# The mix of five paths: its weighing moved from GpSimd to VectorE

## The chip, the cores and the metric

The kernel runs on one core of one Trainium2 chip. The metric is the device time of one execution in microseconds (us), taken as the median of several runs. Engines: TensorE (PE, with its weight loads as PEld), VectorE (DVE), ScalarE (ACT), GpSimd (POOL) and SyncE (SP), which here only issues transfers. Each engine works through its own queue in order; the queues meet in semaphores.

## The reference

A layer on x of shape (2, 1024, 256): a spiking front, a gated attention, a recurrence and a mixture of experts. The change lies in the end of the attention, which for each of 2048 tokens and each of 4 heads mixes five paths of 64 values with weights from a softmax, normalizes, and projects:

```python
probs = jax.nn.softmax(logits / tau[:, None], -1)
eps = jax.nn.sigmoid(eps_logit) * 0.2
probs = probs * (1.0 - jnp.sum(eps, -1, keepdims=True)) + eps
o = jnp.einsum('blhp,blhpd->blhd', probs, paths)
o = o * jax.lax.rsqrt(jnp.mean(o * o, -1, keepdims=True) + 1e-05) * norm_w
return o.reshape(b, Ln, D) @ Wo
```

The logits come from a small network on the hidden states and on four statistics of each path (mean, mean square, mean absolute value, norm).

## The kernel before, in words

The function `mix` treats the tokens as 16 tiles of 128 (a = 0 to 15), four of them to a chunk (n = 0 to 3, TILES = 4, CHUNKS = 4). `m.path[:, a]` holds for one tile 128 tokens x 5 paths x 256 values, so 1280 values in each partition. Each engine has its own list of steps; nothing but the order in these lists and the semaphores decides what runs when.

VectorE, for a tile: `sums` (L1353) makes the statistics; three reductions, over 512 values each for tiles 0 to 11 (part of their statistics was made earlier) and over 1280 for tiles 12 to 15. For a chunk: `scores` (L1363) and `probs` (L1378) make the softmax around ScalarE's exp and leave the weights in `pr[n % 2]`, releasing `probs_ready`. `combine` (L1394) waits for the tile's weighing (`weighted`) and adds the five weighted paths in three additions (L1398, L1400, L1404), releasing `mixed`. `squares` (L1406), `normed` (L1415) do the normalization around ScalarE's Square and Sqrt (`root`, L1186), and `residual` (L1426) adds the projected result to x.

GpSimd, before: nothing but the weighing. For each tile it waits for its chunk's `probs_ready` and multiplies the tile's 1280 values by the weights in place (L1158).

The order on VectorE is written out: in round i, the sums of chunk i + 1, then combine, squares and normed of chunk i - 1, then residual of chunk i - 2, then scores(i) and probs(i). So between probs(n) and combine of chunk n lie, for n = 0 and 1, the twelve reductions of chunk n + 2. For n = 2 nothing lies between. After the last round comes a tail: combine(12), combine(13), residual(2), squares(3), combine(14), combine(15), normed(3), squares(4), normed(4), residual(3), residual(4). From PARTS = ((0, 4), (4, 8), (8, 12), (12, 14), (14, 16)), squares, normed, root, project and residual take chunk 3 in two parts, numbered 3 and 4.

ScalarE in round i: `st_out` (L1168, copies the transposed statistics of chunk i), four `gelu` with the squares of the next chunk between them, `turned_back(i - 2)` (copies for the projection), `norm`, `root(i - 1)`, and the exp of chunk i. Its tail: turned_back(2), zw_out(0), rows_out(0), root(3), zw_out(1), rows_out(1), root(4) and so on.

TensorE in round i: `hidden(i)` (needs st_out(i)), `project(i - 2)`, `logits(i)` (L1277, writes `lg_bank` for scores(i)). Its tail: project(2), gate_part(0), rows(0), gate_part(1), rows(1), project(3), gate_part(2), rows(2), project(4), rows(3), gate_part(3). project(x) transposes the normalized part (L1290) and multiplies by Wo (L1299); gate_part (L1313) and rows (L1329) prepare the recurrence that follows. The recurrence begins when all engines have finished `mix`.

Of the kernel before, what the change touches and what calls it, by code (L numbers as in the profile page):

```python
# [15 lines left out]
ALU = mybir.AluOpType  # L16
# [3 lines left out]
P = 128  # L20
# [3 lines left out]
H, DV = 4, 64  # L24
NP = 5
# [8 lines left out]
CHUNKS = T // CH  # L34
# [1040 lines left out]
def mix(nc, d, m):  # L1075
# [8 lines left out]
    TILES = N // P  # L1084
    CHUNKS = B * T // N
# [5 lines left out]
    with ExitStack() as own:  # L1091
# [11 lines left out]
        pr = [sb(f"pr{i}", [P, TILES, H, NP]) for i in range(2)]  # L1103
# [16 lines left out]
        s = namedtuple("MixSemaphores", names)(*(sem("m_" + n) for n in names))  # L1120
        row_bank = (st_bank, lg_bank)
        path = lambda a: m.path[:, a]
# [3 lines left out]
        block = own.enter_context(nc.Block())  # L1126

        @block.sync
        def _(sp):
            for x in (*m.done_in_project, *m.done_in_fir):  # L1130
                sp.sem_clear(x)
            sp.dma_start(b2[:], d.gb2.partition_broadcast(P)).then_inc(s.g_in, 16)
            sp.dma_start(w2[:], d.gW2.rearrange("(f p) n -> p f n", p=P)).then_inc(s.g_in, 16)
            sp.dma_start(wo[:], d.Wo.rearrange("(c p) n -> p c n", p=P)).then_inc(s.g_in, 16)
            for h in range(P // DV):
                sp.dma_start(nw[h * DV:(h + 1) * DV, :], d.norm_w.unsqueeze(1)).then_inc(s.g_in, 16)
            for c in range(C):
                sp.dma_start(m.xT[:, c * B:(c + 1) * B, :], d.xT[c * P:(c + 1) * P]).then_inc(s.x_in, 16)
            sp.dma_start(m.bias_g[:], d.bg).then_inc(s.wg_in, 16)
            sp.dma_start(m.alpha[:], d.alpha).then_inc(s.wg_in, 16)  # L1140
            sp.dma_start(m.h_start[:], d.condT.rearrange("(c p) b -> p c b", p=P)).then_inc(s.wg_in, 16)
            sp.wait_ge(s.hid_psum, 4 * CHUNKS)
            sp.dma_start(m.wg, d.wgT.rearrange("(k p) n -> p k n", p=P)).then_inc(s.wg_in, 16)
            for i in range(2 * CHUNKS):
                sp.wait_ge(s.row_ready, i + 1)
                sp.dma_start(m.z_rows[2 * i * P:2 * (i + 1) * P, :].rearrange("(a p) n -> p a n", p=P),
                             stage[:, i, :].rearrange("p (a n) -> p a n", n=D)).then_inc(s.rows_out, 16)
            sp.wait_ge(s.x_in, 16 * C)
            sp.wait_ge(s.rows_out, 16 * 2 * CHUNKS)

        @block.gpsimd
        def _(pool):
            for a in range(CHUNKS * TILES):
                n, k = divmod(a, TILES)
                x = path(a).rearrange("q p (h v) -> q p h v", v=DV)
                w = pr[n % 2][:, k].rearrange("q h p -> q p h").unsqueeze(3).broadcast_to([P, NP, H, DV])
                pool.wait_ge(s.probs_ready, n + 1)
                nc.gpsimd.tensor_tensor(x, x, w, ALU.mult).then_inc(s.weighted, 1)  # L1158

        @block.scalar  # L1160
        def _(act):
            def square(a):
# [189 lines left out]
        def _(dve):  # L1352
            def sums(a):  # L1353
                now = late(a)
                at = lambda x: g.st[:, a, x:x + PH].rearrange("q (p h) -> q p h", h=H)[:, now.start:]
                x = path(a)[:, now.start:].rearrange("q p (h v) -> q p h v", v=DV)
                nc.vector.tensor_reduce(at(0), x, AX.X, ALU.add)
                nc.vector.tensor_reduce(at(64), x, AX.X, ALU.add, apply_absolute_value=True)
                dve.wait_ge(s.sq_ready, a + 1)
                nc.vector.tensor_reduce(at(32), sq[:, a % 2, now.start:].rearrange("q p (h v) -> q p h v", v=DV), AX.X,  # L1360
                                        ALU.add).then_inc(s.sq_sums, 1)
# [16 lines left out]
            def probs(n):  # L1378
                rows = lambda x: x[:].rearrange("q t h p -> q t (h p)")
                each = lambda x: x[:].unsqueeze(1).broadcast_to([P, TILES, PH])  # L1380
                flat = lambda x: x[:].rearrange("q t h p -> q (t h) p")
                dve.wait_ge(s.exp_ready, n + 1)
                nc.vector.tensor_reduce(top[:], flat(lg), AX.X, ALU.add).then_inc(s.soft, 1)
                dve.wait_ge(s.soft, SOFT * n + 4)
                nc.vector.reciprocal(top[:], top[:]).then_inc(s.soft, 1)
                dve.wait_ge(s.soft, SOFT * n + 5)
                nc.vector.tensor_tensor(flat(lg), flat(lg), top[:].unsqueeze(2).broadcast_to([P, TILES * H, NP]),
                                        ALU.mult).then_inc(s.soft, 1)
                dve.wait_ge(s.soft, SOFT * n + 6)
                nc.vector.tensor_tensor(rows(lg), rows(lg), each(g.keep), ALU.mult).then_inc(s.shifted, 1)  # L1390
                dve.wait_ge(s.shifted, 2 * n + 2)
                nc.vector.tensor_tensor(rows(pr[n % 2]), rows(lg), each(g.eps), ALU.add).then_inc(s.probs_ready, 1)  # L1392

            def combine(a):  # L1394
                n, k = divmod(a, TILES)
                x = path(a)
                dve.wait_ge(s.weighted, a + 1)
                nc.vector.tensor_tensor(x[:, 0:2], x[:, 0:2], x[:, 2:4], ALU.add).then_inc(s.adding, 1)  # L1398
                dve.wait_ge(s.adding, 2 * a + 1)
                nc.vector.tensor_tensor(x[:, 0], x[:, 0], x[:, 1], ALU.add).then_inc(s.adding, 1)  # L1400
                dve.wait_ge(s.adding, 2 * a + 2)
                if n >= 2:
                    dve.wait_ge(s.ot_psum, TILES * (n - 1))
                nc.vector.tensor_tensor(o[n % 2][:, k, :], x[:, 0], x[:, NP - 1], ALU.add).then_inc(s.mixed, 1)  # L1404

            def squares(x):  # L1406
                a0, a1 = PARTS[x]
                k0, k1 = a0 % TILES, (a1 - 1) % TILES + 1
                dve.wait_ge(s.squared, x + 1)
                if x:  # L1410
                    dve.wait_ge(s.root_ready, x)
                nc.vector.tensor_reduce(ms[:, k0 * H:k1 * H], o2[:, k0:k1].rearrange("q t (h v) -> q (t h) v", v=DV), AX.X,
                                        ALU.add).then_inc(s.ms_ready, 1)

            def normed(x):  # L1415
                a0, a1 = PARTS[x]
                n, k0, k1 = a0 // TILES, a0 % TILES, (a1 - 1) % TILES + 1
                r = rs[:, k0 * H:k1 * H]
                dve.wait_ge(s.root_ready, x + 1)
                nc.vector.reciprocal(r, r).then_inc(s.rs_ready, 1)  # L1420
                dve.wait_ge(s.rs_ready, x + 1)
                y = o[n % 2][:, k0:k1].rearrange("q t (h v) -> q (t h) v", v=DV)
                nc.vector.tensor_tensor(y, y, r.unsqueeze(2).broadcast_to([P, (k1 - k0) * H, DV]),
                                        ALU.mult).then_inc(s.on_ready, 1)

            def residual(x):  # L1426
                a0, a1 = PARTS[x]
                b, t0 = divmod(a0 * P, T)
                cols = slice(a0 % TILES * P, ((a1 - 1) % TILES + 1) * P)
                dve.wait_ge(s.x_in, 16 * C)  # L1430
                for c in range(C):
                    z = m.xT[:, c * B + b, t0:t0 + (a1 - a0) * P]
                    dve.wait_ge(s.wo_psum, C * x + c + 1)
                    nc.vector.tensor_tensor(z, z, wo_bank[c][:, cols], ALU.add).then_inc(s.z_ready, 1)
# [6 lines left out]
            for i in range(CHUNKS):  # L1441
                if i + 1 < CHUNKS:
                    for k in range(TILES):
                        sums((i + 1) * TILES + k)
                if i:
                    for k in range(TILES):
                        combine((i - 1) * TILES + k)
                    squares(i - 1)
                    normed(i - 1)
                if i >= 2:  # L1450
                    residual(i - 2)
                scores(i)
                probs(i)
            combine(12)
            combine(13)
            residual(2)
            squares(3)
            combine(14)
            combine(15)
            normed(3)  # L1460
# [620 lines left out]
def layer_kernel(nc, ins, out):  # L2081
    d = namedtuple("Inputs", ins)(**ins)
    with ExitStack() as ctx:
# [20 lines left out]
        with ExitStack() as attn:  # L2104
# [27 lines left out]
            with ExitStack() as delta:  # L2132
# [5 lines left out]
                fir(nc, d, m)  # L2138
                attend(nc, d, m)
            mix(nc, d, m)  # L2140
        m.middle.close()
        m.h = sb("h", [P, J, 1 + T])
# [41 lines left out]
```

## Time and profile before

| | before |
|---|---|
| median of 3 runs | 1011.98 us |
| lowest and highest run | 1008.6 and 1013.66 us |
| profiled execution: time, span | 1012.18 us, 1010.4 us |
| TensorE, VectorE, ScalarE, GpSimd busy | 734.7, 659.2, 514.4, 257.7 us |
| GpSimd busy with the weighing | 38.7 us, 16 instructions |
| the mix in the span | about 457 to 596 us |

The span is what the engines' records cover; the profiled execution's own time is 1.8 us longer. All start times below count from the span's start. Busy shares are means over the whole kernel and say little about the mix, which has to be read by stretches and by timelines.

### The profile page before, as it was taken

The numbers are of one execution on the slowest core, as the hardware profiler recorded it, in microseconds if no ns is written. First come the engines' busy times: TensorE is split into PE (matmuls) and PEld (weight loads), VectorE is DVE, ScalarE is ACT, GpSimd is POOL, SyncE is SP. The second block draws the span as 40 slices with busy tenths as digits, with TensorE's granted clock in tenths as the row PEclk, the third lists the DMA queues.
The fourth block names the chain that finished last, engine by engine and source line by source line (L and its number), as shares of the span: only waits on it lengthen the run. The fifth ranks groups of instructions, "written<-read, shape, count | busy, mean of one in ns | idle before, by whom it ended". The sixth has DMA issues, their size and how long they took to land. (4 is left out here: it accounts for less than half of the span.)

```text
span 1010.4 us, 15121 instructions
## 1 busy us (share of the span) xinstructions
PE 734.7 (73%) x5694; PEld 459.1 (45%) x5694; DVE 659.2 (65%) x947; ACT 514.4 (51%) x842; POOL 257.7 (26%) x231
## 2 busy tenths in 40 slices
PE   3830019787675387866887789999947599999995
PEld 1310005334565376753444444444416356667773
DVE  5999968877655985465897719999981323333331
ACT  6878745555132445555444359999950113222221
POOL 0000000001102000000333308989870123443331
PEclk9975559899899578997888799999975589999997
DMA  5720000003970000002000144000009511111100
GB/s 213 245 82 0 0 4 18 1 0 101 258 179 6 2 3 24 3 2 96 1 1 21 42 177 198 1 1 0 1 1 292 183 36 36 44 42 39 40 12 1
DMA packets 35882, 60.69 MB, mean 60 GB/s; under 512 B 8187, under 2 KB 22523, under 8 KB 35426
## 3 DMA queue, kind: packets, MB, share of 16 engines
q1 hardware_dynamic: 30194, 51.31, 15.9%
q0 software_dynamic: 3312, 6.31, 2.1%
q10 hardware_dynamic: 2304, 2.10, 0.6%
q8 instruction: 47, 0.77, 0.3%
q14 instruction: 25, 0.20, 0.1%
HBM read 55.23 MB, written 7.21 MB: 62 GB/s over the span
## 5 line engine op out<-in xcount | busy, mean ns | idle before, releaser
L1926 ACT ACTIVATE xT<-x_tr,moe_b 128x128 f32<-128x128 f32 x184 | 50.0, 382 | 147.2 <-PE x_tr L1891 147.2
L1873 PE MATMUL x_hid<-w,moe_xt 128*128 x184 | 85.9, 611 | 0.9 <-DVE moe_xt L2016 0.7
L1882 PE MATMUL x_y<-moe_w,xT 128*128 x368 | 85.0, 385 | 2.1 <-ACT xT L1926 2.1
L1158 POOL TENSOR_TENSOR path<-path,mix_pr 128x1280 f32<-128x1280 f32 x16 | 38.7, 2448 | 146.1 <-DVE mix_pr L1392 146.1
L1882 PEld LDWEIGHTS x_y<-moe_w,xT 128*128 128x128 f32 x368 | 69.4, 193 | 11.6 <-issue 2.8
L2023 DVE COPY xT<-x_hid 128x512 f32<-128x512 f32 x46 | 31.8, 692 | 64.7 <-PE x_hid L1873 64.7
L216 PE MATMUL bad_sum<-spike_bad,ones 128*128 128x16 f32 x2 | 0.6, 384 | 86.8 <-ACT spike_outside L182 86.8
L1547 PE MATMUL r_bank<-recur_h_other,w1h 128*128 128x512 f32 x128 | 60.3, 593 | 0.7 <-ACT recur_h_other L1571 0.7
L1543 PE MATMUL r_bank<-hs,eye 128*128 128x512 f32 x112 | 57.2, 592 | 1.8 <-DVE h L1638 1.8
L474 DVE SCALAR_TENSOR_TENSOR proj_y<-proj_pre,mix_st,proj_y 128x1024 f32<-128x1024 f32 x36 | 46.2, 1284 | 10.9 <-ACT proj_y L437 9.8
L212 PE MATMUL w_bank<-spike_wbuf,spike_pick 128*128 128x512 f32 x80 | 37.9, 624 | 21.1 <-DMA spike_wbuf<-in_gW 21.0
L2031 DVE TENSOR_TENSOR moe_y<-x_y,moe_zin 128x256 f32<-128x256 f32 x23 | 9.8, 425 | 65.8 <-PE x_y L1882 65.8
L1820 POOL DMA_INDIRECT out<-moe_y,slot_token x23 | 23.5, 1022 | 109.2 <-DVE moe_y L2033 109.2
L1873 PEld LDWEIGHTS x_hid<-w,moe_xt 128*128 128x128 f32 x184 | 34.2, 196 | 36.2 <-issue 36.2
L1617 POOL TENSOR_TENSOR recur_rest<-recur_step,recur_h_other 128x512 f32<-128x512 f32 x32 | 37.8, 1180 | 46.0 <-ACT recur_step L1581 45.4
L389 PE MATMUL pj<-hs,mix_st 128*128 128x512 f32 x96 | 45.6, 621 | 2.3 <-PEq L64 2.3
L1547 PE MATMUL r_bank<-h,w1h 128*128 128x512 f32 x96 | 45.1, 592 | 0.0
L1645 DVE TENSOR_TENSOR r_bank<-r_bank,xT 128x512 f32<-128x512 f32 x56 | 38.1, 680 | 8.1 <-ACT r_bank L1577 8.1
L1591 ACT ACTIVATE r_bank<-r_bank,recur_leak,recur_leak_neg 128x512 f32<-128x512 f32 x56 | 42.0, 750 | 1.9
L648 DVE COPY path<-fir_z_bank 64x256 f32<-64x256 f32 x64 | 27.0, 422 | 21.5 <-PE fir_z_bank L583 20.0
L216 PEld LDWEIGHTS bad_sum<-spike_bad,ones 128*128 128x128 f32 x2 | 0.5, 309 | 87.6 <-ACT spike_outside L182 87.6
L160 ACT ACTIVATE spike_count<-spike_line,spike_mid 128x2048 int16<-128x2048 f32 x8 | 39.1, 4886 | 1.1 <-DVE spike_line L243 1.1
(285 smaller groups left out, 1855.4 us busy)
## 6 DMA issues: line engine op xcount, KB each, us to landing
spike_wbuf<-in_gW SPq DMA_DIRECT2D x8, 1280.0 KB, 6.2
w<-in_w1T SPq DMA_DIRECT2D x8, 1024.0 KB, 12.0
moe_w<-in_w2T SPq DMA_DIRECT2D x8, 1024.0 KB, 11.9
fir_band<-in_band_l SPq DMA_DIRECT2D x11, 512.0 KB
fir_band<-in_band_m SPq DMA_DIRECT2D x11, 312.0 KB
mix_st<-in_band_l SPq DMA_DIRECT2D x5, 512.0 KB
xT<-in_xT SPq DMA_DIRECT2D x4, 512.0 KB, 5.7
xT<-in_xT SPq DMA_DIRECT2D x2, 1024.0 KB, 6.1
```

What stands on the lines that cost most here:

```text
L160: nc.scalar.activation(count[i][:, 2:].rearrange("p (t s) -> p s t", s=SUB), line[u % 2][:], ACT.Relu, bias=mid[:]).then_inc(rounded, 1)
L212: last = nc.tensor.matmul(w_bank[:], pick[:, at:at + P], wbuf[:, ch % 2, i, :], start=(ch == 0 and i == 0), stop=(ch == CHUNKS - 1 and i = ...
L389: last = nc.tensor.matmul(pj[u % 2][:, n * N:(n + 1) * N], w[:, i, k, c * P:(c + 1) * P], m.hs[:, k * B + b, n * N:(n + 1) * N], start=(k ...
L474: nc.vector.scalar_tensor_tensor(out, pre[:, u % 2, k:k + T], wc[:, i, c, k:k + 1], out, ALU.mult, ALU.add).then_inc(conv_step if k < KQ - ...
L1158: nc.gpsimd.tensor_tensor(x, x, w, ALU.mult).then_inc(s.weighted, 1)
L1543: nc.tensor.matmul(out, m.eye[:], zw[:, c * B + b, t0:t0 + N], start=True, stop=False)
L1547: last = nc.tensor.matmul(out, wg[:, k, c * P:(c + 1) * P], state[u // UNITS % 2][:, k * B + b, t0:t0 + N], start=False, stop=(k == C - 1))
L1591: nc.scalar.activation(out, out, ACT.Identity, bias=leak[:, c:c + 1], scale=leak_neg[:, c:c + 1]).then_inc(s.j_ready, 1)
L1645: nc.vector.tensor_tensor(x, x, m.xT[:, c * B + b, t0:t0 + N], ALU.mult).then_inc(s.gz_ready, 1)
L1873: last = nc.tensor.matmul(hid_bank[n][:], xt[:, c, :], m.w1[:, bass.ds(e, 1), c, n * N:(n + 1) * N].rearrange("p o n -> p (o n)"), start=( ...
L1882: last = nc.tensor.matmul(y_bank[:], ht[:, k, :], w2[:, bass.ds(e, 1), k, :].rearrange("p o n -> p (o n)"), start=(k == 0), stop=(k == K2 ...
L1926: nc.scalar.activation(ht[:, k, :], tr_bank[k // (K2 // 2)][:, k % (K2 // 2) * P:(k % (K2 // 2) + 1) * P], ACT.Relu, bias=b1[:, bass.ds(e, ...
```

## The change

The block of GpSimd in `mix` is gone. A new step `weigh(a)` on VectorE does the same multiply with the same operands, and is called for the four tiles of a chunk right in front of their combine; in the tail for two tiles at a time. Nothing else is moved. `combine` still waits for `weighted`, which VectorE itself now releases.

```diff
-        @block.gpsimd
-        def _(pool):
-            for a in range(CHUNKS * TILES):
-                n, k = divmod(a, TILES)
-                x = path(a).rearrange("q p (h v) -> q p h v", v=DV)
-                w = pr[n % 2][:, k].rearrange("q h p -> q p h").unsqueeze(3).broadcast_to([P, NP, H, DV])
-                pool.wait_ge(s.probs_ready, n + 1)
-                nc.gpsimd.tensor_tensor(x, x, w, ALU.mult).then_inc(s.weighted, 1)
-
...
+            def weigh(a):
+                n, k = divmod(a, TILES)
+                x = path(a).rearrange("q p (h v) -> q p h v", v=DV)
+                w = pr[n % 2][:, k].rearrange("q h p -> q p h").unsqueeze(3).broadcast_to([P, NP, H, DV])
+                dve.wait_ge(s.probs_ready, n + 1)
+                nc.vector.tensor_tensor(x, x, w, ALU.mult).then_inc(s.weighted, 1)
+
...
                 if i:
                     for k in range(TILES):
+                        weigh((i - 1) * TILES + k)
+                    for k in range(TILES):
                         combine((i - 1) * TILES + k)
...
+            weigh(12)
+            weigh(13)
             combine(12)
             combine(13)
             residual(2)
             squares(3)
+            weigh(14)
+            weigh(15)
             combine(14)
             combine(15)
             normed(3)
```

## Rows read from the trace of the kernel before

**Rows 1.** The page: busy time of the engines, and the weighing's group.

```profile
PE 734.7 (73%) x5694; PEld 459.1 (45%) x5694; DVE 659.2 (65%) x947; ACT 514.4 (51%) x842; POOL 257.7 (26%) x231
...
L1158 POOL TENSOR_TENSOR path<-path,mix_pr 128x1280 f32<-128x1280 f32 x16 | 38.7, 2448 | 146.1 <-DVE mix_pr L1392 146.1
```

**Rows 2.** Busy time by stretches: PE, PEld, DVE, ACT, POOL, then clock, DMA.

```profile
480.00:505.00 25.00, 20.66 (x69) 10.69 (x68) 20.45 (x45) 12.33 (x19) 9.35 (x4) 0.85 0.00 1
505.00:536.00 31.00, 22.59 (x77) 11.73 (x76) 28.61 (x39) 14.76 (x21) 9.36 (x4) 0.83 0.00 1
536.00:559.00 23.00, 19.92 (x76) 11.19 (x74) 18.12 (x26) 9.05 (x17) 9.98 (x4) 0.87 0.07 23
```

**Rows 3.** Timeline of GpSimd: start, us, what, idle before it.

```profile
505.19 9.36 POOL L1158 TENSOR_TENSOR path<-path,mix_pr 128x1280 f32<-128x1280 f32 x4 [12.99 <-DVE mix_pr L1392]
536.07 9.98 POOL L1158 TENSOR_TENSOR path<-path,mix_pr 128x1280 f32<-128x1280 f32 x4 [21.52 <-DVE mix_pr L1392]
```

**Rows 4.** Timeline of VectorE, 491 to 571 us.

```profile
491.66 1.08 DVE L1398 TENSOR_TENSOR path<-path 128x512 f32<-128x512 f32 x1
...
520.35 1.48 DVE L1360 TENSOR_REDUCE mix_st<-mix_path_sq 128x20 f32<-128x1280 f32 x1
521.74 0.68 DVE L1398 TENSOR_TENSOR path<-path 128x512 f32<-128x512 f32 x1
...
527.49 0.42 DVE L1404 TENSOR_TENSOR mix_o<-path 128x256 f32<-128x256 f32 x1
...
535.75 0.24 DVE L1392 TENSOR_TENSOR mix_pr<-mix_lg,mix_eps 128x80 f32<-128x80 f32 x1
538.47 2.84 DVE L1398 TENSOR_TENSOR path<-path 128x512 f32<-128x512 f32 x1 [2.48 <-POOL path L1158]
...
543.86 2.48 DVE L1404 TENSOR_TENSOR mix_o<-path 128x256 f32<-128x256 f32 x1
...
550.47 0.42 DVE L1404 TENSOR_TENSOR mix_o<-path 128x256 f32<-128x256 f32 x1
...
556.26 0.23 DVE L1368 TENSOR_TENSOR mix_lg<-lg_bank,mix_gb2r 128x80 f32<-128x80 f32 x1
...
570.77 1.28 DVE L1434 TENSOR_TENSOR xT<-xT,wo_bank 128x512 f32<-128x512 f32 x2
```

**Rows 5.** VectorE's groups by form: busy us, mean ns, idle before.

```profile
L467 DVE TENSOR_SCALAR proj_y<-proj_pre,mix_st 128x1024 f32<-128x1024 f32 x8 | 5.9, 736 | 8.6 <-ACT proj_pre L433 8.6
L957 DVE STREAM_TRANSPOSE w1h<-delta_raw 128x1024 f32<-128x1024 f32 x2 | 3.8, 1912 | 3.4 <-ACT delta_raw L870 3.4
L1357 DVE TENSOR_REDUCE mix_st<-path 128x20 f32<-128x1280 f32 x4 | 5.9, 1478 | 0.0
L1423 DVE TENSOR_TENSOR mix_o<-mix_o,mix_rs 128x1024 f32<-128x1024 f32 x3 | 3.7, 1225 | 0.1
```

**Rows 6.** Timeline of TensorE, 535 to 577 us.

```profile
535.13 2.08 PE L1267 MATMUL hid_bank<-mix_st_t,w1s 128*128 128x512 f32 x2 [7.43 <-ACT mix_st_t L1170]
...
551.24 3.64 PE L1277 MATMUL lg_bank<-mix_gw,mix_gel 128*128 128x20 f32 x32
...
559.50 5.05 PE L1299 MATMUL wo_bank<-mix_o_t,mix_wo 128*128 128x512 f32 x8 [0.46 <-ACT mix_o_t L1203]
564.39 3.60 PE L1313 MATMUL hid_bank<-xT,w1h 128*128 128x512 f32 x8
...
576.57 1.12 PE L1290 MATMUL ot_bank<-eye,mix_o 128*128 128x128 f32 x4 [3.40 <-DVE mix_o L1423]
```

**Rows 7.** Timeline of ScalarE, the last copy of rows_out(0).

```profile
569.08 0.60 ACT L1218 COPY mix_z_stage<-lg_bank 128x512 f32<-128x512 f32 x1
```

**Rows 8.** TensorE by short stretches: us, busy, then the granted clock.

```profile
532.00:535.00 3.00, 0.00 (x0) 0.50 0.00 0
537.00:539.00 2.00, 2.00 (x5) 0.66 0.00 0
580.00:582.00 2.00, 2.00 (x6) 0.50 0.00 0
```

## The prediction

> **What bounds the kernel now.** I read the page first, for the size of the thing that moves: GpSimd's sixteen weighings take 38.7 us in all, 2448 ns each [rows 1]. The page's chain of waits covers only the end of the kernel, so it says nothing of this stage. I therefore cut the mix into stretches by VectorE's probs results and asked for each engine's busy time in each [rows 2]. In 480:505 and 505:536 VectorE is busy 20.45 of 25 us and 28.61 of 31 us and GpSimd only 9.35 and 9.36; in 536:559 VectorE still shows 18.12 of 23 us, but that figure has to be taken apart, because it holds waiting. The timelines do it. In chunks 0 and 1 the weighing runs beside VectorE's sums and is finished long before combine asks for it: chunk 1's weighing ends at 505.19 + 9.36 = 514.55 us [rows 3], and VectorE reaches combine at 521.74 [rows 4]. So there VectorE sets the pace and GpSimd is hidden. In chunk 2 no sums are left. VectorE is free at 535.99 (535.75 + 0.24), waits 2.48 us for the first weighing, and of its next three additions the first and the third take 2.84 and 2.48 us where the same ones take 0.68 and 0.42 elsewhere [rows 4]. Each of the three ends about with one of GpSimd's four instructions [rows 3]: the two engines keep each other out. The combine of chunk 2 ends at 550.89 (550.47 + 0.42), 14.9 us after probs. The tail with chunk 3 repeats this at its start: combine(12) and (13) together end at 570.77 [rows 4]. Thus the profile has two halves: two chunks whose weighing costs nothing, and two whose weighing costs much.
>
> **The price of one weighing on VectorE.** Before has no such instruction, a tensor_tensor over 128x1280 with one operand of step 0 inside. The nearest rows are the sums over the same 1280 elements, 1478 ns, and normed's multiply, also with an operand repeated 64 times, 1225 ns for 1024 [rows 5]; 256 elements more at the same pace (1225 / 1024 = 1.2 ns) make 1.5 us. What the queue pays is the distance between starts: a 1280-element sum starts at 520.35 and the next instruction at 521.74, 1.39 us [rows 4]. I take 1.40, four for 5.6 us. The bounds: a one-source 128x1024 operation takes 736 ns, which is 0.92 for 1280; a transpose of 1024 takes 1912 ns, which is 2.39 for 1280 [rows 5]. I take the value near the middle since its rows have the same size and the same kind of operand.
>
> The Trainium skill ("VectorE: DVE Perf Modes", The DRAIN you can't avoid) says that the next VectorE instruction doesn't start until the pipe is empty; with 1.48 us for 1.40 the sum below would be under 1 us higher. The row of two starts 1.39 us apart doesn't bear it out.
>
> **The sum, by VectorE's order.** All times in the frame of before; "shift" is how late things are by then.
>
> Chunk 0: after the second round of sums VectorE starts combine(0) at 491.66. Four weighings come in front, +5.6. The first addition took 1.08 instead of 0.68 because GpSimd was still busy [rows 4], -0.4. Nothing hides the 5.2: squares, normed, scores(1), probs(1) are all behind it on VectorE, ScalarE's exp waits for scores, and its copy st_out(2) behind exp holds TensorE's hidden(2). Shift 5.2.
>
> Chunk 1: the same in front of combine(4), without a clash to win back, +5.6. Shift 10.8.
>
> Chunk 2: combine alone takes 6.16 us for four tiles (521.74 to 527.49 + 0.42) [rows 4]. With 5.6 of weighing it is 11.76 against 14.9: VectorE is done at 547.7, 3.2 us sooner. Then it meets TensorE: scores(3) needs logits(3), which end at 551.24 + 3.64 = 554.88 [rows 6], and before it started at 556.26 [rows 4]. Only 1.35 of the 3.2 come through. Shift 9.45; VectorE should wait nearly 2 us at scores(3).
>
> Tail: in a frame 1.35 us earlier, probs(3) is done at 557.64; weighing tiles 12 and 13 takes 2.8, combining them 3.1, so they are ready at 563.6 where before had 570.77 [rows 4]. After residual(2) (1.2) VectorE stands at squares(3) from 564.8. This needs ScalarE's Square in root(3), which is queued behind zw_out(0) and rows_out(0); these hang on TensorE's project(2) and gate_part(0) (559.50 and 564.39) [rows 6] and their last copy ended at 569.68 (569.08 + 0.60) [rows 7]. Moved by 1.35 it ends at 568.3, Square at 568.9. So VectorE waits some 4 us at squares(3); then 0.6 for that, 2.8 for the weighing of tiles 14 and 15, 3.1 for their combine, and 0.9 for normed(3), making 576.25. Before, TensorE's project(3) started at 576.57 after waiting 3.40 us for exactly this result [rows 6]. The tail thus starts 0.3 us sooner than before: of some 6 us that the clash gives back there, the wait for ScalarE and the second pair of weighings take nearly all. From there to the recurrence it is TensorE's and ScalarE's work, unchanged.
>
> Sum: 5.2 + 5.6 - 0.3 = +10.5 us. No transfer changes: the load of the gate weights waits for hidden(3), and the rows of z leave after the copies, both simply later. GpSimd's removed instructions free nothing before the recurrence, where its work waits for ScalarE. The profiled execution of before took 1012.18 us, the median of the runs is 1011.98; so 1022.7 by the one, **1022.5** by the other.
>
> **The rivals.**
> 1. TensorE's clock. Near the end of a wait of 7.43 us it stood at its lower level, 1.2 GHz (granted 0.50, 532:535), and with work again since 535.13 it was at 0.66 in 537:539; after a wait of only 3.40 us it was still at 0.50 in 580:582 [rows 6, 8]. The change makes the wait inside hidden(2) 5.2 us longer and the one inside hidden(3) 5.6, to 13.0 us. If low clock lasts some 3 us more in chunk 3 and again in the tail, each costs half, 1.5 us: +13.5, 1025.5. For it: logits(3) is now on the path. Against: the low stretch doesn't grow with the wait in these rows. In the other direction, project(2) took 5.05 us for eight matmuls of the same size as gate_part(0)'s eight behind it, which took 3.60 [rows 6]; it comes sooner after logits(3), and if it then takes 3.6 too, the total falls to 1021.1.
> 2. Stepped or repeated operand slow on VectorE, 2.4 us a weighing: chunks 0 and 1 cost 9.2 and 9.6, chunk 2 gains nothing (+0.9), the tail ends 3.9 late in all: +22.7, 1034.9. At 0.92 us: 3.3 + 3.7 - 1.4 = +5.6, 1017.6. The multiply of normed speaks against both.
> 3. The waits for TensorE and ScalarE in chunk 3 and the tail don't appear, so that all of the clash comes back: 16 x 1.40 = 22.4 added, 0.4 + 2 x 8.8 = 18 returned (14.9 - 6.16 = 8.8 each): +4.4, 1016.4. Against it stands the order of both queues.
> 4. Faster: the weighings of chunks 0 and 1 are hidden in waits of VectorE, and the gains of chunks 2 and 3 (8.8 - 5.6 = 3.2 each) count in full: -6.4, 1005.6. With the full gains it turns faster once more than 4.4 of the 10.8 us are hidden, with the gains of my sum only past 10.5. VectorE is idle 4.55 us in 480:505 and 2.39 in 505:536 [rows 2], in pieces between dependent steps, which says no.
> 5. Weighing sets the time wherever it is done, so that the faster engine wins: sixteen times 2.4 - 1.4 us, -16, 996. The rows of chunks 0 and 1 say that it is hidden there. The Trainium skill ("GPSIMD Engine Reference", Engine selection) gives such work to VectorE, GpSimd being about two times slower with two inputs. The rows agree on the ratio (2.4 against 1.4), but not on what follows for a queue that is already full.
>
> **How the numbers follow.** Forecast (with its small variant of project(2)) 0.71, its own range 1019.5 to 1024.5; longer low clock 0.13; slow operand 0.06, quick operand 0.02; full return 0.04; hidden weighings 0.03; weighing as the bound 0.01. The range 1018 to 1027 covers the first two and the runs' own scatter of a few us. A kernel with runs from 1008.6 to 1013.7 can't tell less than 0.5% (5 us) from no change; the limits are 1006.9 and 1017.0. Faster 0.04, same 0.04 (full return), slower 0.92.
>
> **What would show it.** VectorE: sixteen multiplies of about 1.48 us, all additions of combine back at 0.68 and 0.42 us, total busy about 659 + 23.7 - 13 = 670 us; GpSimd 219. probs(1), (2), (3) end 5.2, 10.8 and about 9.4 us later than before. A wait of about 2 us for lg_bank at scores(3), about 4 us for ScalarE's Square at squares(3), TensorE's project(3) 10.5 us later. The recurrence then has before's times with one shift. Wrong would be: a weighing far from 1.4 us; a probs(2) less than 9 us late, which would mean slack on VectorE that I don't see; or a stretch after 610 us that is itself longer or shorter.

## The result, and the profile after

| | before | after |
|---|---|---|
| median of the runs | 1012.51 us (4 runs) | 1023.59 us (4 runs, 1021.95 to 1026.24) |
| ratio | | 1.0108, 95% interval 1.0079 to 1.0136 |
| profiled execution: time, span | 1012.18, 1010.4 us | 1021.95, 1020.1 us |
| probs(0) to the recurrence (VectorE's starts) | 114.13 us | 124.87 us |
| from there to the end of the span | 413.76 us | 412.77 us |

The change makes the kernel 1.1% slower. The fourth row is the one to work with. It runs from the start of the last instruction of probs(0), up to which both kernels do the same, to the start of VectorE's copy into `recur_leak_j`, the third of its first instructions in the recurrence: 10.74 us more, where 10.5 was forecast.

The page of after, its busy line, and VectorE's groups by form from 480 to 607 us (busy us, mean ns, idle before), against [rows 1, 5]:

```profile
PE 730.0 (72%) x5694; PEld 454.3 (45%) x5694; DVE 670.2 (66%) x963; ACT 514.4 (50%) x842; POOL 218.6 (21%) x215
```

```profile
L1390 DVE TENSOR_TENSOR path<-path,mix_pr 128x1280 f32<-128x1280 f32 x16 | 22.8, 1484 | 0.1
L1396 DVE TENSOR_TENSOR path<-path 128x512 f32<-128x512 f32 x16 | 10.9, 683 | 0.0
L1402 DVE TENSOR_TENSOR mix_o<-path 128x256 f32<-128x256 f32 x16 | 6.8, 425 | 0.6
```

A weighing takes 1484 ns on VectorE, and all the additions are back at 683 and 425 ns: none of them waits inside itself for GpSimd any more. VectorE's busy time grew by only 11.0 us though 16 instructions were added, since the stretched additions of before had counted as busy.

VectorE's timeline (start, us, what, idle before it), against [rows 4]:

```profile
491.61 5.68 DVE L1390 TENSOR_TENSOR path<-path,mix_pr 128x1280 f32<-128x1280 f32 x4
```

```profile
497.21 0.68 DVE L1396 TENSOR_TENSOR path<-path 128x512 f32<-128x512 f32 x1
...
510.00 0.24 DVE L1383 TENSOR_TENSOR mix_pr<-mix_lg,mix_eps 128x80 f32<-128x80 f32 x1
...
525.49 1.47 DVE L1351 TENSOR_REDUCE mix_st<-mix_path_sq 128x20 f32<-128x1280 f32 x1
532.49 0.68 DVE L1396 TENSOR_TENSOR path<-path 128x512 f32<-128x512 f32 x1
...
546.48 0.24 DVE L1383 TENSOR_TENSOR mix_pr<-mix_lg,mix_eps 128x80 f32<-128x80 f32 x1
...
558.11 0.42 DVE L1402 TENSOR_TENSOR mix_o<-path 128x256 f32<-128x256 f32 x1
560.70 1.22 DVE L1410 TENSOR_REDUCE mix_ms<-mix_o 128x16 f32<-128x1024 f32 x1 [2.17 <-ACT mix_o L1183]
...
566.99 0.24 DVE L1359 TENSOR_TENSOR mix_lg<-lg_bank,mix_gb2r 128x80 f32<-128x80 f32 x1 [1.96 <-PE lg_bank L1268]
...
575.62 1.28 DVE L1432 TENSOR_TENSOR xT<-xT,wo_bank 128x512 f32<-128x512 f32 x2
580.54 0.69 DVE L1410 TENSOR_REDUCE mix_ms<-mix_o 128x8 f32<-128x512 f32 x1 [3.64 <-ACT mix_o L1183]
```

Four weighings lie between the last sum and the first addition: 497.21 - 491.61 = 5.6 us. In chunk 1 the sum at 525.49 is followed by nothing but another four (532.49 is 7.0 us later, 1.4 of it the sum). In chunk 2 combine ends 11.8 us after probs(2) (558.53 - 546.72) where before took 14.9. The wait of 2.17 us behind it stands in before too, with 1.12 us. Then two new waits stand in the list, for lg_bank and, in the tail, for ScalarE's Square. TensorE's timeline shows why the first is there (against [rows 6]):

```profile
545.87 2.08 PE L1258 MATMUL hid_bank<-mix_st_t,w1s 128*128 128x512 f32 x2 [13.73 <-ACT mix_st_t L1161]
547.74 3.62 PE L1255 MATMUL hid_bank<-hs,w1h 128*128 128x512 f32 x4
551.15 1.34 PE L1258 MATMUL hid_bank<-mix_st_t,w1s 128*128 128x512 f32 x2
...
563.30 3.64 PE L1268 MATMUL lg_bank<-mix_gw,mix_gel 128*128 128x20 f32 x32
...
570.11 4.75 PE L1290 MATMUL wo_bank<-mix_o_t,mix_wo 128*128 128x512 f32 x8 [0.46 <-ACT mix_o_t L1194]
574.69 3.60 PE L1304 MATMUL hid_bank<-xT,w1h 128*128 128x512 f32 x8
...
587.96 1.11 PE L1281 MATMUL ot_bank<-eye,mix_o 128*128 128x128 f32 x4 [4.49 <-DVE mix_o L1421]
```

And the clock of the same stretch (us, busy, then the granted clock; 0.50 is 1.2 GHz, 1.00 is 2.4), against [rows 8]:

```profile
540.00:545.00 5.00, 0.00 (x0) 0.50 0.00 0
545.00:547.00 2.00, 1.13 (x2) 0.50 0.00 0
547.00:549.00 2.00, 2.00 (x4) 0.50 0.00 0
549.00:551.00 2.00, 2.00 (x3) 0.50 0.00 0
551.00:553.00 2.00, 2.00 (x5) 0.81 0.00 0
```

Work began again at 545.87 and the clock was still low at 551; before it had begun at 535.13 and was rising within 537:539. So four matmuls took 3.62 us, and logits(3) ended late (563.30 + 3.64 = 566.94, just ahead of scores(3) at 566.99).

### The profile page after: what moved, and what is told of

It is laid out like the page before. It is cut to its first block and busy times, and to the rows that moved or that the text cites. A ratio compares the mean times of both kernels' runs of the same rounds, so it can differ in the third digit from the quotient of the medians.

```text
span 1020.1 us, 15121 instructions
## 1 busy us (share of the span) xinstructions
PE 730.0 (72%) x5694; PEld 454.3 (45%) x5694; DVE 670.2 (66%) x963; ACT 514.4 (50%) x842; POOL 218.6 (21%) x215
## 5 line engine op out<-in xcount | busy, mean ns | idle before, releaser
L1886 PEld LDWEIGHTS x_y<-moe_w,xT 128*128 128x128 f32 x368 | 68.2, 190 | 11.1 <-issue 2.8
L474 DVE SCALAR_TENSOR_TENSOR proj_y<-proj_pre,mix_st,proj_y 128x1024 f32<-128x1024 f32 x36 | 46.2, 1284 | 11.1 <-ACT proj_y L437 10.0
L1551 PEld LDWEIGHTS r_bank<-recur_h_other,w1h 128*128 128x128 f32 x128 | 24.4, 192 | 32.3 <-issue 30.8
```

Of the source, the lines that this page charges most:

```text
L474: nc.vector.scalar_tensor_tensor(out, pre[:, u % 2, k:k + T], wc[:, i, c, k:k + 1], out, ALU.mult, ALU.add).then_inc(conv_step if k < KQ - ...
L1551: last = nc.tensor.matmul(out, wg[:, k, c * P:(c + 1) * P], state[u // UNITS % 2][:, k * B + b, t0:t0 + N], start=False, stop=(k == C - 1))
L1886: last = nc.tensor.matmul(y_bank[:], ht[:, k, :], w2[:, bass.ds(e, 1), k, :].rearrange("p o n -> p (o n)"), start=(k == 0), stop=(k == K2 ...
```

## The experiments

In the expectations v_late and so on are the names of the kernels told here. All traces are read in one way, from the start of the last instruction of probs(0) (0 in the table): probs(2) and scores(3) are starts on VectorE, "recurrence" the copy named above. Starts count from there because the stages ahead of the mix end up to 5.5 us apart from one execution to the next. The ratio is to runs of before on the same chip.

| kernel | probs(2) | scores(3) | recurrence | ratio, 95% interval |
|---|---|---|---|---|
| before | 53.24 | 73.75 | 114.13 | |
| after (the full change) | 64.02 | 84.53 | 124.87 | 1.0108, 1.0079 to 1.0136 |
| v_early | 62.38 | 82.89 | 122.34 | 1.0101, 1.0068 to 1.0134 |
| v_late | 53.25 | 72.35 | 114.23 | 1.0018, 0.9989 to 1.0047 |
| late_dve | 53.26 | 72.58 | 111.31 | 0.9986, 0.9967 to 1.0005 |
| v_tail | 53.23 | 72.29 | 108.84 | 0.9970, 0.9944 to 0.9997 |
| v_tail_again | 53.26 | 72.31 | 108.87 | 0.9970, 0.9951 to 0.9989 |
| all_tail | 64.07 | 83.08 | 119.63 | 1.0068, 1.0043 to 1.0092 |
| before_order | 53.24 | 73.75 | 116.15 | 1.0013, 0.9990 to 1.0037 |
| no_overlap | 53.24 | 74.48 | 114.89 | 0.9999, 0.9981 to 1.0017 |
| warm | 62.35 | 88.16 | 129.06 | 1.0173, 1.0127 to 1.0219 |
| warm14 | 64.05 | 81.63 | 121.95 | 1.0120, 1.0072 to 1.0169 |
| tail_warm | 53.23 | 72.52 | 109.07 | 0.9982, 0.9957 to 1.0008 |

**v_early: chunks 0 and 1 alone on VectorE.** GpSimd's list of before comes back for tiles 8 to 15.

```diff
+            for a in range(8, 16):
...
+                    for k in range(TILES) if i <= 2 else ():
                         weigh((i - 1) * TILES + k)
```

> Only chunks 0 and 1 are weighed on VectorE, chunks 2 and 3 on GpSimd as before. My theory (VectorE's queue is full there, nothing hides the weighing): probs(2) ends about 10.8 us later than before's 535.99 and nothing is given back, because the clash in chunks 2 and 3 stays; with TensorE's longer low clock in chunk 3 hidden behind VectorE. Time before + 10.8 us, so about 1.1% slower, the same or a little more than the full change. Rival (the two chunks are partly hidden, the full change loses its time in chunks 2 and 3): less than + 5 us.

By its runs the kernel can't be told from the full change (1.0101 and 1.0108). In the trace probs(2) is 9.14 us late, not 10.8, and the recurrence 8.2 us, not 10.8. Chunk 1 costs what was said (36.50 us from probs(1) to probs(2), before 30.88, so 5.62); chunk 0 costs 3.52 (25.88 to probs(1), before 22.36). The missing 1.66 us are a wait of before that isn't there in this execution, and it is TensorE's clock. It shows in warm too, which is the full change up to that place. Clock of after, then of warm:

```profile
476.00:480.00 4.00, 3.83 (x34) 1.00 0.00 0
480.00:482.00 2.00, 2.00 (x6) 0.52 0.00 0
```

```profile
476.00:480.00 4.00, 3.80 (x34) 1.00 0.00 0
480.00:482.00 2.00, 2.00 (x9) 1.00 0.00 0
```

With the high clock the squares that VectorE's sums wait for come sooner. VectorE's timeline of v_early where the weighing begins:

```profile
488.09 5.69 DVE L1399 TENSOR_TENSOR path<-path,mix_pr 128x1280 f32<-128x1280 f32 x4
```

That is 7.45 us after probs(0), in after 9.15 us, and combine(0) of before starts 9.15 us after it too: the difference lies ahead of everything that the change touches. From there to probs(1) v_early takes 18.43 us, after 18.39 and before 13.21. So the step costs 5.2 us in both. All eight executions with the weighing of chunk 0 on GpSimd have the longer way to probs(1) (22.35 to 22.37 us), none the high clock's shorter one, so the 3.52 us compare unlike executions.

All of chunk 2's clash is kept (20.51 us from probs(2) to scores(3), to the hundredth as before). Another 0.95 us is missing behind TensorE's project(3): from there to project(4) are 9.02 us, in before 9.97. The theory stands for the place of the loss, the rival (under 5 us) falls.

**v_late: chunks 2 and 3 alone on VectorE.** GpSimd's list is `range(8)`, and the loop weighs where i > 2.

> Only chunks 2 and 3 are weighed on VectorE, chunks 0 and 1 on GpSimd as before. My theory: the clash is gone, combine of chunk 2 ends 3.2 us earlier, but scores(3) waits for logits(3) and only 1.35 us come through; in the tail squares(3) waits some 4 us for ScalarE's Square, and TensorE's project(3) starts only 0.3 us earlier than before's 576.57. Time before - 0.3 us, no difference that can be measured. Rival (all of the clash comes back once chunks 0 and 1 don't pay): - 6.4 us, 0.6% faster. Second rival (low clock of TensorE after the longer wait costs the full change its gain in chunk 3): here the wait is as long as before, so scores(3) is 1.35 us early, and in the full change it was 0.05 us early.

Nothing gained: the recurrence is 0.1 us later than before, expected 0.3 earlier. scores(3) comes 1.4 us sooner as expected, and the two waits stand where they should:

```profile
554.83 0.24 DVE L1368 TENSOR_TENSOR mix_lg<-lg_bank,mix_gb2r 128x80 f32<-128x80 f32 x1 [1.59 <-PE lg_bank L1277]
```

```profile
569.45 0.69 DVE L1419 TENSOR_REDUCE mix_ms<-mix_o 128x8 f32<-128x512 f32 x1 [4.71 <-ACT mix_o L1192]
570.05 2.88 DVE L1399 TENSOR_TENSOR path<-path,mix_pr 128x1280 f32<-128x1280 f32 x2
```

VectorE does nothing for 4.71 us and then, behind the wait, the two weighings for which it had had all it needed. The rival (-6.4 us) falls. The second rival (a longer low clock after the longer wait takes the full change's gain in chunk 3) fits v_late and after, but not all_tail below.

**late_dve: the second pair of weighings into the wait.**

```diff
             residual(2)
-            squares(3)
             weigh(14)
             weigh(15)
+            squares(3)
```

> v_late with VectorE's part of the tail order alone: the weighing of tiles 14 and 15 in front of squares(3), ScalarE's order as before. squares(3) still waits for ScalarE until about 569, but the second weighing now lies in that wait: TensorE's project(3) starts 2.9 us earlier than in v_late (measured from probs(0): 94.4 us there, about 91.5 here), and the time is about 3 us below v_late's. Rival (ScalarE's wait is all that matters): no gain without ScalarE's order.

The recurrence comes 2.92 us sooner than in v_late; project(3) starts at 91.93 instead of 94.39, 2.5 us sooner (2.9 expected). The rival falls. By whole runs 0.14% faster than before is not clear of the scatter.

**v_tail: ScalarE's order too.** Beside the edit of late_dve:

```diff
             turned_back(2)
+            root(3)
             zw_out(0)
             rows_out(0)
-            root(3)
             zw_out(1)
             rows_out(1)
+            turned_back(3)
             root(4)
-            turned_back(3)
```

> As v_late, with two queue orders of the tail changed: on VectorE the weighing of tiles 14 and 15 stands in front of squares(3), and on ScalarE root(3) stands in front of zw_out(0) and rows_out(0), and turned_back(3) in front of root(4). My theory (the gain of the tail is lost in the wait at squares(3) for ScalarE and in the second pair of weighings behind it): the wait at squares(3) goes, normed(3) is done about 572.2, TensorE's project(3) starts 4.4 us earlier than before, its clock stays high; time before - 4.5 to - 5 us. Rival (the tail is bound by TensorE's own work whatever VectorE does): as v_late, within 1 us.

> v_tail once more, in more rounds, to see whether it is faster than before clear of the scatter (the first time: 0.9970, interval 0.9944 to 0.9997). My theory: from probs(0) to the recurrence 108.8 us against before's 114.1, so 0.5% faster. Rival: the profiled execution was a lucky one, the ratio is within 0.2% of 1.

VectorE's and TensorE's timelines of v_tail:

```profile
561.32 2.88 DVE L1399 TENSOR_TENSOR path<-path,mix_pr 128x1280 f32<-128x1280 f32 x2
564.12 0.68 DVE L1419 TENSOR_REDUCE mix_ms<-mix_o 128x8 f32<-128x512 f32 x1
```

```profile
569.80 0.60 PE L1329 MATMUL lg_bank<-eye,xT 128*128 128x128 f32 x4
570.24 0.60 PE L1290 MATMUL ot_bank<-eye,mix_o 128*128 128x128 f32 x4
571.81 1.99 PE L1299 MATMUL wo_bank<-mix_o_t,mix_wo 128*128 128x256 f32 x8 [0.98 <-ACT mix_o_t L1203]
```

squares(3) waits for nothing, and project(3) follows rows(1) without a pause, where before TensorE had waited 3.40 us [rows 6]. The recurrence comes 5.3 us earlier than in before, twice. The path there isn't quite the expected one. normed(3) is done 89.5 us after probs(0), as was said, but TensorE reaches project(3) only behind rows(1), 91.04 us after probs(0): 3.0 us sooner than in before, where 4.4 were expected. The other 2.3 us are won between project(3) and project(4), 7.71 us where before took 9.97; the granted clock is 1.00 there (569 to 585 us), in before it was 0.50 in 577:581. By the runs the kernel is 0.3% faster than before, both times with an interval below 1; the trace's 5.3 of 1012 us would be 0.9948, inside the first interval and just outside the second.

**all_tail: the full change with v_tail's orders.**

> The full change with both queue orders of the tail changed as in v_tail. If the tail's gain is lost in the same two places in the full change, the time from probs(3) to the recurrence's first copy falls from 37.84 us to about 34.0, as in v_tail (554.00 to 588.04), and the whole time by 4 to 5 us below the full change's, which leaves it some 6 us above before. Rival (in the full change something else holds the tail): no more than 1 us.

From probs(3) to the recurrence 34.05 us, after 37.84. The gain of the tail is lost in the same two places in the full change. The further 1.5 us by which it beats after lie ahead of scores(3), which came at 83.08. Up to there the two kernels do the same. TensorE's timeline and clock in all_tail tell them apart:

```profile
547.09 2.08 PE L1258 MATMUL hid_bank<-mix_st_t,w1s 128*128 128x512 f32 x2 [13.54 <-ACT mix_st_t L1161]
548.96 2.40 PE L1255 MATMUL hid_bank<-hs,w1h 128*128 128x512 f32 x4
551.20 1.02 PE L1258 MATMUL hid_bank<-mix_st_t,w1s 128*128 128x512 f32 x2
```

```profile
549.00:551.00 2.00, 2.00 (x5) 0.75 0.00 0
551.00:553.00 2.00, 2.00 (x6) 1.00 0.00 0
```

After a rest as long as in after (13.54 us, there 13.73) the clock is back at 2.4 GHz by 551, about 4 us into the work, where after was still at 0.50 more than 5 us into it. From probs(2) to scores(3) all_tail takes 19.01 us, 1.50 less than before: what the forecast had for chunk 2 (1.35).

**before_order: ScalarE's order without the change.** The same edit of ScalarE's list, nothing else.

> Before, with ScalarE's order of the tail alone changed as in v_tail (root(3) in front of zw_out(0) and rows_out(0), turned_back(3) in front of root(4)). With the weighing on GpSimd the combine of tiles 12 and 13 ends only at 570.77, so root(3) now holds zw_out(0) back, and TensorE's gate_part(1) behind it: time before + 2 us. Rival (the order of ScalarE is what made v_tail faster, wherever the weighing is): - 3 to - 5 us.

+2.02 us to the recurrence in the trace; the runs (1.0013, interval 0.9990 to 1.0037) can't tell it from before. The rival falls: the order of ScalarE is worth something only with a combine that ends early. The 2 us are what is left of more: project(3) starts 4.27 us later than in before, and between project(3) and project(4) 2.25 us are won back (7.72 us where before took 9.97). gate_part(1) waits as was said, for the copies (zw_out) that now stand behind root(3):

```profile
572.05 6.26 PE L1313 MATMUL hid_bank<-xT,w1h 128*128 128x512 f32 x8 [5.12 <-ACT hs L1212]
```

**no_overlap: how much the two engines share.**

```diff
-                dve.wait_ge(s.weighted, a + 1)
+                dve.wait_ge(s.weighted, a + 1 if n < 2 else TILES * (n + 1))
```

> Before, but in chunks 2 and 3 the first combine waits until GpSimd has weighed all four tiles of the chunk. If the two engines keep each other out, starting the additions early bought next to nothing: GpSimd's four take 9.36 us as in chunks 0 and 1 instead of 9.98, all additions take 0.68 and 0.42, combine of chunk 2 ends at about 551.6 instead of 550.89, and the whole time is 0.5 to 1.5 us longer. Rival (they share, and the additions of the first tile ran beside the weighing): 3 us or more longer.

GpSimd's and VectorE's timelines:

```profile
537.32 9.35 POOL L1158 TENSOR_TENSOR path<-path,mix_pr 128x1280 f32<-128x1280 f32 x4 [21.53 <-DVE mix_pr L1392]
```

```profile
546.70 0.69 DVE L1398 TENSOR_TENSOR path<-path 128x512 f32<-128x512 f32 x1 [9.46 <-POOL path L1158]
547.42 0.42 DVE L1400 TENSOR_TENSOR path<-path 128x256 f32<-128x256 f32 x1
```

With the additions held back until GpSimd had finished, chunk 2 is 0.73 us longer, the whole stretch 0.76, and the runs don't show it. In before [rows 4] not only the first and the third addition were stretched, the second was too:

```profile
541.34 2.48 DVE L1400 TENSOR_TENSOR path<-path 128x256 f32<-128x256 f32 x1
```

The three did 1.52 us of work (0.68, 0.42 and 0.42) in 7.80, and GpSimd's four weighings were stretched from 9.35 to 9.98 us beside them. For the most part the two had been taking turns.

**warm, warm14: TensorE kept at work in the wait of hidden(3).** After with additional matmuls, 26 and 13:

```diff
+                    if n == 3 and f == 0:
+                        pe.wait_ge(s.ot_ready, 4)
+                        for _ in range(13):
+                            nc.tensor.matmul(ot_bank[0][:], g.w1h[:, 0, 0:P], m.hs[:, b, t0:t0 + N], start=True, stop=True)
                     pe.wait_ge(s.st_ready, n + 1)
```

> The full change, with 26 additional matmuls of TensorE (results not used) in hidden(3), in the wait for st_out(3) that grew from 7.43 to 13.73 us, so that TensorE doesn't stand still there. If the low granted clock after that wait is what made scores(3) 1.3 us later than forecast (566.99 where 565.71 was forecast), scores(3) comes 1.3 us earlier here, at about 565.7, and the recurrence starts up to 1.3 us earlier; the whole time is 0 to 1.5 us below the full change's. Rival (something else is late, or the tail takes it back): no change of the recurrence's start, 607.05.

A miss of mine: each matmul goes in two passes, so that the 26 took 22.48 us and overran the wait. It says nothing of the clock as a cause of lateness, and was mended:

> The full change, with 13 additional matmuls of TensorE (each in two passes, results not used) in the wait of hidden(3): 26 passes of 0.43 us are 11.2 us and fit into the wait of 13.73 us, where the 52 passes of the run before (22.48 us) overran it. If low granted clock after the wait made scores(3) late, the time from probs(2) to scores(3), 20.51 us in the full change, falls by 1.3 us here to about 19.2, and the time from probs(0) to the recurrence's first copy falls by 0 to 1.3 us. Rival (the clock is not the cause): 20.5 us as before.

TensorE in warm14:

```profile
532.45 11.32 PE L1260 MATMUL ot_bank<-hs,w1h 128*128 128x512 f32 x26
546.13 1.12 PE L1262 MATMUL hid_bank<-mix_st_t,w1s 128*128 128x512 f32 x2 [2.37 <-ACT mix_st_t L1161]
547.09 1.88 PE L1255 MATMUL hid_bank<-hs,w1h 128*128 128x512 f32 x4
```

The six matmuls behind the wait take 1.12 and 1.88 us instead of 2.08 and 3.62. scores(3) comes 17.58 us after probs(2), 2.9 us sooner than in after and 1.6 sooner than I expected, because the low stretch that before has too is gone with the rest. 2.93 us against before's 20.51 is nearly the whole 3.2 us that the clash gives back in chunk 2. The recurrence comes 2.92 us sooner than in after. By the runs the two can't be told apart, and all_tail shows that 1.5 of the 2.9 us can also come without a warmed TensorE.

**tail_warm: the same in v_tail**, with 7 matmuls.

> v_tail with 7 additional matmuls of TensorE (two passes each, 14 x 0.43 = 6.0 us, results not used) in hidden(3)'s wait of 7.44 us. In v_tail scores(3) waits 1.55 us for TensorE's logits(3), whose work began at low clock. With the clock held up scores(3) comes 1.5 us after the time it has in v_tail less, so 70.8 us after probs(0) instead of 72.3, and since TensorE sets the pace of the tail, the recurrence starts about 1.5 us sooner, 107.3 us after probs(0) instead of 108.84; time 0.15% below v_tail's. Rival (as in the full change with the 13 matmuls only chunk 3 gains and the tail takes it back): 108.8.

```profile
527.91 6.17 PE L1269 MATMUL ot_bank<-hs,w1h 128*128 128x512 f32 x14
536.90 2.01 PE L1271 MATMUL hid_bank<-mix_st_t,w1s 128*128 128x512 f32 x2 [2.82 <-ACT mix_st_t L1170]
538.71 2.73 PE L1264 MATMUL hid_bank<-hs,w1h 128*128 128x512 f32 x4
```

No gain, and not for the rival's reason: after 2.82 us of rest the granted clock was 0.50 in 537:539, just as work had begun, where in warm14, after 2.37 us, it was 1.00 in 545:549. v_tail stays the fastest kernel of this study.

## Why the prediction was right

The mechanism of chunks 0 and 1, which is the whole of the loss, was right and right in size. The total of +10.74 us for +10.5 owes something to luck all the same: chunk 2 gave 1.35 us less than forecast, the tail cost 1.05 us less, and the sum hadn't foreseen that the two would cancel. The stages as the two traces have them (us more than before):

| step of the sum | forecast | measured |
|---|---|---|
| chunk 0, to probs(1) | +5.2 | 27.54 - 22.36 = +5.18 |
| chunk 1, to probs(2) | +5.6 | 36.48 - 30.88 = +5.60 |
| chunk 2, to scores(3) | -1.35 | 20.51 - 20.51 = 0.0 |
| tail, to the recurrence | +1.05 (-0.3 in all) | 40.34 - 40.38 = 0.0 |
| sum | +10.5 | +10.74 |

**The price.** 1.40 us between starts and 1.48 for one came out as (497.21 - 491.61) / 4 = 1.40 and 1484 ns. An operand of step 0 inside and of step 5 outside it costs VectorE nothing here (a sum over 1280 elements takes 1478 ns); the slow and the quick operand (rival 2) fall. The Trainium skill ("VectorE: DVE Perf Modes", The DRAIN you can't avoid) has the next instruction wait for an empty pipe, and adds that one which isn't held starts earlier. The trace agrees with the second: the starts lie 0.08 us closer than one instruction lasts.

**Chunks 0 and 1.** Right to 0.02 us in the profiled execution, and v_early has the loss with these two chunks alone. What I took for fixed is the wait in chunk 0's sums: it is there or not with TensorE's clock. It lies ahead of the weighing, so it moves one execution against another by 1.66 us and leaves the price of the step at 5.2.

**Chunk 2.** The mechanism was right (VectorE early, then waiting for logits(3), 1.96 us where nearly 2 were forecast), the size was off: 0.0 for -1.35. In this execution it is rival 1, with a low clock that lasted some 3 us longer than before's; v_late, whose wait is as short as before's, has the -1.4, and warm14, without the low clock, has -2.9. But the longer rest alone doesn't decide it. From the first to the second group of L1258 matmuls after takes 5.28 us (13.73 us of rest) and v_early 5.08 (13.06), while all_tail takes 4.11 (13.54), no more than the 4.15 to 4.43 of the seven executions with 7.4 us of rest. So a longer low stretch came in two of three executions with a long rest; all_tail, the full change up to there, has -1.50. The runs leave open what decides it. In v_early it costs nothing, since its scores(3) hangs on VectorE.

**Tail.** Forecast were a wait of some 4 us at squares(3) (3.64) and project(3) with 0.3 us of the clash's 6 left. Measured from scores(3), project(3) starts 20.97 us later, before 20.31, forecast 21.36. Project(2) took 4.75 us instead of 5.05. The last 0.7 us came behind it: project(3) and gate_part(2) took 3.56 and 3.60 us there, and before 3.78 and 4.11, again by the clock; the forecast had called that stretch unchanged. The two steps belong together: in v_late, with chunk 2 at -1.41, the tail measured +1.50, and its project(2), started sooner after logits(3), took 5.68 us, where the prediction's small variant had 3.6 for a sooner start. late_dve, v_tail and all_tail show that the wait and the order of the two weighings had swallowed the gain.

**The rivals that fell.** Full return (+4.4): v_late. Hidden weighings: v_early. Weighing as the bound, to which the Trainium skill's advice on such work ("GPSIMD Engine Reference", Engine selection) would lead if it is taken for a rule on the whole kernel: VectorE is indeed quicker at it (1.48 against 2.45 us, 1.65 times, where the page has about two), and the kernel is slower.

**Not settled.** From the recurrence on the kernels do the same work, and take from 410.9 (before_order) to 416.1 us (tail_warm) in these executions, with before at 413.8 and after at 412.8. So the profiled executions' difference of 9.8 us and the runs' of 11.1 can't be compared more closely than that. Why TensorE's clock differs between executions, at 480 us and in the work after the long rest, wasn't looked into.

## What to carry to other kernels

Before moving work from a slow engine to a fast one, ask of each place where it lies, not how fast it is: a slow instruction beside a full queue is free, a fast one in that queue costs its whole length. Where the move does clear a clash, look at what is next in line behind it; here the freed time ended in another engine's queue until two lists were put in another order, and half of the places were worth moving and half were not. In a list written by hand, work that is ready belongs in front of a wait, not behind it.

## What the runs showed of the hardware

- VectorE's additions with two inputs in SBUF and GpSimd's multiply hardly run together: three additions worth 1.52 us took 7.80 beside it, and starting them early gained 0.73 us (no_overlap), while VectorE's reductions beside the same multiply keep their 0.68 and 1.48 us, and four multiplies their 9.35.
- TensorE was at 1.2 GHz for nearly all of 480:482 in after (0.52) although it had been busy 3.83 of the 4 us before and went on being busy; in warm, with the same instructions there, it stayed at 2.4. Chunk 0 is 1.66 to 1.68 us shorter with the high clock (v_early, warm).
- 2.37 us of rest behind added matmuls left the granted clock at 1.00 in warm14, 2.82 us in tail_warm did not; one execution of each is no proof of a limit between them.
- After rests of 13.73 (after), 13.06 (v_early) and 13.54 us (all_tail) TensorE's low clock lasted unequally long: the same six matmuls took 5.28, 5.08 and 4.11 us. After and all_tail do the same work up to there, and chunk 2 differs by 1.5 us between them.
